# One list of steps for all head groups, V in 17-column tiles and value products in two parts, in an eight-layer attention kernel

## The reference

```python
# A: the mask multiplies the scores, so masked ones are 0 and still take part in the softmax
scores = jnp.einsum('bthd,bshd->bhts', q, k) * tril
attn = softmax(scores / T ** 0.5); out = attn @ v @ Wo
# B: no mask, two score maps of 8 features each
score = softmax(attn1 - lam * attn2); out = 0.8 * (score @ v) @ W_proj
# C: causal (-inf), plus scores of 64 rotary features that are common to all heads
scores = (ac + ar[:, None]) / sqrt(80); out = softmax(scores) @ v @ Wo
```

## Time and profile before

| | us |
|---|---|
| median of 3 runs | 2836.49 (2823.72 to 2842.88) |
| the profiled execution | 2827.55 |
| its span | 2825.6 |
| TensorE, VectorE, ScalarE, GpSimd busy | 2528.0, 1888.5, 1227.1, 166.2 |
| attention A: maxima from 85, first exponential, end | 156.2, 630 |
| attention B: maxima from 1118, first exponential, end | 1168.8, 1908 |
| attention C: maxima from 2125, first exponential, end | 2187.2, 2749 |

### The profile page before, as it was taken

One profiled execution on the slowest core, in us unless ns is written; L12 is line 12 of the kernel. 1 busy time (PEld: TensorE's weight loads), 2 busy tenths in 40 slices (PEclk: granted clock), 3 DMA queues, 4 the chain that ended last, 5 costly groups with the idle time before them and its releaser, 6 DMA issues. The chain is left out here.

```text
span 2825.6 us, 41425 instructions
## 1 busy us (share of the span) xinstructions
PE 2528.0 (89%) x14390; PEld 1281.6 (45%) x14390; DVE 1888.5 (67%) x4599; ACT 1227.1 (43%) x1494; POOL 166.2 (6%) x386
## 2 busy tenths in 40 slices
PE   6899999989999997999898999996776999999995
PEld 4543434336565564433333333334343555555554
DVE  5578778735445534899898898948556766666718
ACT  3145556561111112266676666681210544445551
POOL 2111111110000000000000000000000100010100
PEclk9759889899999998599999998998865999999997
DMA  6600330000000007100301200000475235252200
GB/s 198 123 1 2 46 38 10 1 17 3 0 1 1 12 1 190 23 1 1 46 1 15 33 1 1 1 1 16 126 248 129 64 72 95 65 105 66 63 1 30
DMA packets 73916, 130.54 MB, mean 46 GB/s; under 512 B 12530, under 2 KB 31730, under 8 KB 70130
## 3 DMA queue, kind: packets, MB, share of 16 engines
q1 hardware_dynamic: 73716, 127.97, 19.9%
HBM read 88.84 MB, written 38.27 MB: 45 GB/s over the span
## 5 line engine op out<-in xcount | busy, mean ns | idle before, releaser
L1126 ACT ACTIVATE PF<-PS 128x1024 f32<-128x1024 f32 (+3 forms) x1152 | 1048.0, 952 | 883.7 <-PE PS L953 497.6
L1340 DVE TENSOR_REDUCE MP<-PS 128x1 f32<-128x512 f32 (+3 forms) x1664 | 988.1, 652 | 198.2 <-PE PS L894 155.4
L894 PE MATMUL PS<-KR,QR 48*128 48x512 f32 (+3 forms) x2304 | 785.3, 492 | 111.2 <-DVE MP L1336 39.5
L894 PEld LDWEIGHTS PS<-KR,QR 48*128 48x128 f32 x2304 | 356.7, 203 | 697.3 <-DVE MP L1340 478.3
L978 PE MATMUL PS<-PF,VG 128*32 128x512 f32 (+3 forms) x4608 | 601.8, 598 | 0.1
L953 PE MATMUL PS<-QR,KR 50*128 50x512 f32 (+3 forms) x2304 | 483.6, 430 | 29.9 <-ACT PF L1126 14.6
L1336 DVE CUSTOM_DVE_ANT_0 JUNK<-PS,WA 128x512 bf16<-128x512 f32 (+3 forms) x512 | 286.4, 605 | 152.8 <-issue 81.1
L953 PEld LDWEIGHTS PS<-QR,KR 50*128 50x128 f32 x2304 | 243.0, 198 | 183.0 <-ACT PF L1126 119.4
L754 PE MATMUL PS<-RQ,RK 64*128 64x512 f32 (+3 forms) x1920 | 259.3, 368 | 0.0
L748 PE MATMUL PS<-HT,WA 128*128 128x512 f32 x512 | 221.1, 592 | 0.0
L754 PEld LDWEIGHTS PS<-RQ,RK 64*128 64x128 f32 x1920 | 186.6, 190 | 24.1
(11 more groups left out here) (143 smaller groups left out, 1431.3 us busy)
## 6 DMA issues: line engine op xcount, KB each, us to landing
WA<-rope_scores SPq DMA_DIRECT2D x88, 256.0 KB, 3.1
rope_scores<-HT SPq DMA_DIRECT2D x28, 256.0 KB, 2.5
WC<-rope_scores SPq DMA_DIRECT2D x24, 256.0 KB, 3.3
QR<-parts_a_q SPq DMA_DIRECT2D x18, 256.0 KB, 11.4
KR<-parts_a_k SPq DMA_DIRECT2D x18, 256.0 KB, 14.4
QR<-parts_b_q SPq DMA_DIRECT2D x18, 256.0 KB, 11.6
KR<-parts_b_k SPq DMA_DIRECT2D x18, 256.0 KB, 14.5
QR<-parts_c_q SPq DMA_DIRECT2D x18, 256.0 KB, 11.7
```

The costliest lines, as they stand in the source:

```text
L894: ins = mm(bank(slots[h][0], w), QR[rows, t0 + tb * P:t0 + (tb + 1) * P], KR[rows, t0 + s0:t0 + s0 + w], start=True, stop=not masked)
L1126: sc.activation(PT[:, u % SETS, 2 * q:2 * q + 2, off:CH], src, ACT.Exp).then_inc(L.exp_done, 1)
L1340: ins = v.reduce_max(MP[:, i, c, y:y + 1], src, AX.X)
```

## The change

The planner makes one list for all four groups (`L.steps`), and all engines have it written out. Units and jobs carry their group. There is no drain at a group's end. How far the maxima have to be by each moment is the upper hull of points (start of a chunk's scores, maxima of that chunk done + `SLACK`), so the maxima run ahead by what the next chunk needs and no more. The costs in the planner are slightly changed.

A unit of more than 256 queries has its value product in two: "half" for the queries below 256 of the chunk stands between the two score pairs, "pv" for the others behind the second pair. Diagonal units of 256 and 128 queries keep one.

V is stored once, in 17 columns a head (16 and a one), and the 32 columns of weights are read right there, into the next head's columns; what comes of those is not used. `VG`, its copies and the waits for them go.

SyncE loads the stacks of groups 2 and 3 in three pieces of four DMAs, at the last value product of the group before and 5 and 10 units later.

```diff
+VW = DH + 1
-MARGIN = 0.04
+STACK_STEP = 5
+SLACK = 9.0
...
+            part = max(0.0, width(k) - 0.5) if k >= 0 else 0.0
             if u < self.n_unit:
...
+                two((0.9 if self.rope else 0.3) * width(u) + 0.1, "score", u, 0)
+            if part:
+                two(1.05 * part + 0.1, "half", k)
+            if u < self.n_unit:
+                two((0.9 if self.rope else 0.3) * width(u) + 0.1, "score", u, 1)
+            if k >= 0:
+                two(1.05 * (width(k) - part) + 0.1, "pv", k)
...
+        points = [(x, min(total, y + SLACK)) for x, y in zip(starts, done_at)] + [(whole, total)]
...
+            while at < len(ones) and given < target(run + cost / 2):
+                given += ones[at][0]
+                steps.append(ones[at][1])
+                at += 1
...
-        VALL = sb("VALL", [P, NB, D])
-        VG = sb("VG", [P, NB, HG, 2 * DH])
+        VO = sb("VO", [P, NB * H * VW + 2 * DH - VW])
+        VALL = VO[:, 0:NB * H * VW].rearrange("p (b h d) -> p b h d", h=H, d=VW)
+        VALUES = VALL[:, :, :, 0:DH]
+        v_tile = lambda b, h: VO[:, (b * H + h) * VW:(b * H + h) * VW + 2 * DH]
...
+                for g in range(2, NG):
+                    for i in range(3):
+                        stacks[(g - 1) * L.n_group - 1 + STACK_STEP * i] = (g, i)
...
+                        load_stacks(L, g, g & 1, pieces=range(i, i + 1))
...
-            constant(g_.memset(VG[:, :, :, DH:2 * DH], 1.0))
+            constant(g_.memset(VO[:], 1.0))
...
-                for i in range(4):
-                    b = slice(quarter * i, quarter * (i + 1))
-                    src = VALL[:, b, bass.ds(g * (HG * DH), HG * DH)].rearrange("p b (j d) -> p b j d", d=DH)
-                    g_.tensor_copy(VG[:, b, :, 0:DH], src).then_inc(L.v_ready, 1)
...
+                    if step[0] in ("half", "pv"):
                         u = step[1]
+                        g, c, sb_, off = L.units[u]
+                        if step[0] == "half":
+                            end = CH // 2
+                        else:
+                            off, end = max(off, CH // 2), CH
...
                         for j in range(HG):
+                            ins = mm(PS[32 * j:32 * j + 2 * DH, 7 * CH + off:7 * CH + end], v_tile(sb_, HG * g + j), PT[:, u % SETS, j, off:end],
+                                     start=first and step[0] == "half", stop=last, tile_position=(0, 32 * j), skip_group_check=True)
+                        if step[0] == "pv":
+                            ins.then_inc(L.pv_done, 1)
```

More of the change, by code:

```diff
@@ L120, in __init__ @@
         self.out_read = s("out_read")
-        self.v_ready = s("v_ready")
         self.chain = s("chain")
     def diagonal(self, u):
-        c, sb, off = self.units[u]
+        _, c, sb, off = self.units[u]
         return self.causal and sb >= BPC * c
     def plan(self):
[L131 to L139, removed]
@@ L140, in plan @@
-        total = sum(x[0] for x in ones)
-        twos = []
+        width = lambda u: (CH - self.units[u][3]) / CH
+        ones, done_at = [], []
+        for n, (g, p, tb, i, s0, w, diag) in enumerate(self.jobs):
+            ones.append(((1.24 if self.rope else 1.14) * w / CH + (0.34 if self.rope else 0.1), ("max", n)))
+            if n + 1 == len(self.jobs) or self.jobs[n + 1][2] // BPC != tb // BPC:
+                cell = g * NC + tb // BPC
+                ones += [(0.35, ("neg", cell)), (0.8, ("mtr", cell))]
+                done_at.append(sum(x[0] for x in ones))
@@ L143, in plan, with two @@
+        total = done_at[-1]
+        twos, starts = [], []
+        run = 0.0
+        def two(cost, *step):
+            nonlocal run
+            twos.append((cost, step))
+            run += cost
         for u in range(self.n_unit + LAG):
+            if u in self.chunk_first:
+                starts.append(run)
+            k = u - LAG
+            part = max(0.0, width(k) - 0.5) if k >= 0 else 0.0
             if u < self.n_unit:
-                twos += [((0.9 if self.rope else 0.25) * width(u) + 0.1, ("score", u, p)) for p in range(NP)]
@@ L152, in plan @@
+        steps, late, run, given, at = [], [], 0.0, 0.0, 0
         for cost, step in twos:
+            while at < len(ones) and given < target(run + cost / 2):
+                given += ones[at][0]
+                steps.append(ones[at][1])
+                at += 1
             if step[0] == "score" and step[1] in self.chunk_first and step[2] == 0:
-                start[self.chunk_first.index(step[1])] = run / whole
-            run += cost
-        lead = max(chunk_end[c] - start[c] * total for c in range(NC)) + MARGIN * total
@@ L157, in plan @@
[L157 to L203, removed]
+                cell = self.chunk_first.index(step[1])
+                while ("mtr", cell) in [x for _, x in ones[at:at + 200]]:
+                    given += ones[at][0]
+                    steps.append(ones[at][1])
+                    at += 1
+                if self.zeros:
+                    if cell == 0:
+                        steps.append(("rest",))
+                    steps.append(("shift", cell))
@@ L204 @@
+            if late and late[0][0] <= run:
+                steps.append(late.pop(0)[1])
+            steps.append(step)
+            run += cost
+            if step[0] == "pv" and step[1] in self.chunk_last:
+                assert not late
+                cell = self.chunk_last.index(step[1])
+                steps.append(("save", cell))
+                late.append((run + 3.0, ("otr", cell)))
+        steps += [x for _, x in ones[at:]]
+        self.steps = steps + [x for _, x in late]
 TAKES = {"max": 2, "mtr": 1, "otr": 1}
@@ L1404, in attention @@
                         dve.wait_ge(ar_out[i], 16 * ar_place.count(i))
[L1405 to L1410 removed]
+                attention_steps(L)
             for kind, steps in PROGRAM:
```

284 lines of the change are left out of this document (132 added, 152 removed).

## The result

The changed kernel took 2880.2 us (median of 6 runs, 2858.2 to 2945.3), the kernel before 2833.2 beside it: a ratio of 1.016, 95% interval 1.012 to 1.021, some 47 us slower. I had forecast 2770 and given 0.09 to slower by over 1%.

What follows compares the result with a forecast made beforehand. Layer B was taken as near VectorE's bound, C as bound by TensorE, A by neither alone. +3 (start) - 30 (A) - 53 + 6 (B) + 8 (C) = -66 gave span 2760, median 2770, range 2700 to 2832.

Steps and rivals of the forecast that it cites:

- Start, +3: Kernel start: the fill of the larger V tile takes longer and delays the first input scaling and transposes, +3 us.
- A, -30: First attention layer: scores start 27 us earlier and group boundaries go, so maxima end at 557 instead of 588, -30 us.
- B's middle, -53: Second attention layer: chunks fall from 45.5 to 43 us, saving 37, and three boundaries save 16; -53 us.
- B's tail, +6: End of layer B: the last chunk's scores wait for the maxima's rows, +6 us; TensorE's 2.0 a unit counted as hidden.
- Without that cover 6 us: B's tail: if ScalarE's 1.96 a unit does not hide TensorE's work, 0.36 a unit, 6 us.
- C, +8: Third attention layer, bound by TensorE: -29 + 5 - 15 - 3 + 4 + 46, +8 us in sum.
- All but the halves: Layer C without the split value products: shorter lead, later jobs, stack loads in pieces, boundaries gone, row wait; -38 us.
- The halves: Layer C: 128 second value products, each adding a change of form at 0.36 us, +46 us (18 to 73).
- a change of form costs 0.72: Slower rival: each half's change of form costs twice the forecast value, A +16, C +54, total 2917 us; chance 0.08.
- A's maxima later than 575: Sign of being wrong: layer A's maxima end later than 575 us, where 557 was forecast.
- a stretch at 0.50: Sign on TensorE's clock: the forecast expected no stretch at 0.50 at the starts of groups 1 to 3.

Runs made afterwards that it cites:

- B's maxima earlier: Changed kernel with layer B's maxima planned to end 12 planned us before its last chunk begins; 2862.9 us over all ten, 1.007 of the kernel before.
- the whole product: Changed kernel with the value product whole again, all 512 queries behind the second score pair; 2810.5 us, 0.990 of the kernel before.
- both halves behind: Changed kernel with both halves of each value product behind the second score pair in all layers, maxima allowed between them; 2752.1 us, 0.973 of the kernel before.
- A alone behind: Changed kernel with both halves behind the second score pair in layer A only, B and C as changed; 2799.1 us, 0.989 of the kernel before.
- the longer lead: Changed kernel with 48 steps instead of 23 ahead of layer A's first score, halves still around the pair; 2897.6 us, 1.020 of the kernel before.

## Why the prediction was wrong, point by point

- **Start, +3:** right. The fill of the V tile took 3.74 us and all behind it came 2.8 later.
- **A, -30:** the step that failed. The first exponential came at 132.16, as forecast (129 + 3). The time of the maxima was then priced at 1.17 us for each us of VectorE, from the rate of the kernel before, and that rate was one at mostly full clock. Measured over the same 358.6 us of VectorE, against 1.19 for my 1.17 with its 8 us: 1.61 and 1.57 in the two profiles of the changed kernel (132 to 711 in the first), 1.45 in the profile of the kernel with B's maxima earlier, 1.30 with the whole product (to 598), 1.22 with both halves behind (to 569). So the price was too low even without halves: the early start ran into the lower clock, and its 27 us were lost soon: the sixth save came at 335.5 with the whole product, at 323.2 before. The rest, 69 to 81 us in medians, is the halves' place. So A did not gain 30 us; it lost 124 in the profile and an estimated 60 to 75 in the median. The term for A held nothing for a TensorE that stays at 0.50. I had seen stretches at 0.50 and took them for something that a boundary causes and that passes.
- **B's middle, -53:** right in size. Chunks of 42.9 against my 43; from the first chunk's maxima to the last 660.8 us against 709.7, -49 (-54 and -55 in the kernels with A alone behind and with the longer lead; -34 in the first profile, whose first two chunks took 61 and 52 us). The mechanism is borne out as well: without maxima between the halves the gain is gone.
- **B's tail, +6:** wrong by its cover. The row wait was there (6.6 us), but I let ScalarE's 1.96 a unit hide TensorE's 2.0. At the lower clock TensorE took 3.47 a unit, and the tail from the last maxima to the last save 66 us instead of 43. "Without that cover 6 us" was priced at full clock.
- **C, +8:** the sum came out nearly (-3 to +3 in six profiles of this C), but in part by luck, since two terms were off in opposite ways. All but the halves, for which I had -38: -30, read from the whole product. The halves: +27 to +33 for my +46. The two waits of some 8 us for a score tile are gone, as said (VectorE's waits for tiles fell from 39.8 us to 25.4 and 23.7). The unit of the tail took 3.41 for my 3.4, and the pause stands before each half as said; where maxima stood among the units less of it was paid.
- **The rivals:** "a change of form costs 0.72" gave 2917, a time near the profiled one, but by another mechanism, with A at +16. A change of form costs 0.36 at full clock (C's tail) and 0.46 at the lower (3.47 against 3.01, one unit of B's tail). The missing rival was a TensorE that stays at its lower clock because of the order. The signs that I gave for being wrong (A's maxima later than 575, a stretch at 0.50) were the ones that showed it.

The mechanism of my gain was right, and a different place keeps it: both halves behind the second pair, maxima allowed between them, halves around the pair only in B's middle. That version is at 2740, 3.4% below the kernel before (0.966, 0.959 to 0.974).

Not settled: what in the one list makes A lose an estimated 60 to 75 us (124 in the profile) with halves around the pair where the old structure lost 33. It is not the lead. In both profiles of the changed kernel no wait of TensorE's loads between 132 and 680 us is longer than 1.93 us, so B's account, by one long pause, is not shown for A. That the halves' place decides is shown for A; that too little streaming between the changes of form is the reason is shown in B's tail and only argued for A. The 17-column tiles of V, the pacing and the stack loads in pieces were never taken apart: all together, without halves, they are worth 1.0% (0.990).

## What to carry to other kernels

An order that fills the gaps of one engine by cutting another's work into more changes of form has to be priced at both of TensorE's clock levels, and every cover ("hidden behind ScalarE") checked at the lower one. Look in the profile of before for stretches at 0.50 and ask what brings the clock up again; if the new order thins out TensorE's work there, the loss can be many times the cost of the change itself. Cutting a long product where it stands, and letting other work in between, gave most of the gain (2752 us, against 2741 with the halves around the pair in B's middle) without that cost.

## What the runs showed of the hardware that I had not expected

- TensorE stayed at clock 0.50 for 54 us while its records show it busy for all of them, in one order, and rose to 1.00 in the same place once the order changed, or once more matmuls were issued in the same order.
- Issuing 704 needless matmuls made the kernel 40 to 51 us faster (2869 to 2880 against 2829). In B's tail, where it gave 10, the clock's rise is seen.
- A value product of 512 queries cut into two of 256 that follow each other costs nothing in C's tail (3.05 us a unit either way); I had put at least 0.14 on the cut. In B, with nothing issued between the parts, a chunk took 0.5 us more (47.1 against 46.6).
